# mLSTM cross-attention and spiking FFN: another order of all steps, and normalisation offsets column by column

## What is computed

```python
def _mlstm_cell(q, k, v, ...):              # q = layernorm(x), k = v = ctx
    ifg = concatenate([q, k, v], -1)
    ig, fg = ifg @ igate_w.T + igate_b, ifg @ fgate_w.T + fgate_b   # 8 heads
    cs = cumsum(log_sigmoid(fg), 1)
    log_D = where(tril, cs[:, :, None] - cs[:, None, :], -inf) + ig[:, None, :]
    m = max(log_D, -1)
    C = (qh @ kh.T) / sqrt(32) * exp(log_D - m)
    h = C / (maximum(abs(C.sum(-1)), exp(-m)) + 1e-6) @ vh
    return layernorm(h) * ln_scale
x = x + tanh(g_xattn) * _mlstm_cell(layernorm(x), ctx, ctx)

def _L0_ffn_ref(x):                         # x = layernorm(x)
    y = square(relu(x @ W_fc.T)) @ W_proj.T             # 256 -> 1024 -> 256
    # 5 steps: mem = 0.9 * mem + y - (mem > 1); spikes += (mem_new > 1)
    return sum(spikes) / 5
x = x + tanh(g_ffn) * _L0_ffn_ref(layernorm(x))
```

## Time and profile before

| | |
|---|---|
| median of 3 runs | 650.81 us (650.64 to 652.63) |
| profiled execution | 652.49 us |
| its span in the trace | 650.7 us |
| busy: PE / DVE / POOL / ACT | 90% / 83% / 75% / 74% |
| mean granted clock of TensorE | 0.978 |
| moved by DMA | 71.33 MB, 110 GB/s |

### The profile page before, as it was taken

One profiled execution on the slowest core, in us unless ns is written; L12 is line 12 of the kernel. 1 busy time (PEld: TensorE's weight loads), 2 busy tenths in 40 slices (PEclk: granted clock), 3 DMA queues, 4 the chain that ended last, 5 costly groups with the idle time before them and its releaser, 6 DMA issues.

```text
span 650.7 us, 17665 instructions
## 1 busy us (share of the span) xinstructions
PE 586.0 (90%) x6032; PEld 483.9 (74%) x6032; DVE 540.4 (83%) x1222; ACT 483.0 (74%) x1011; POOL 485.6 (75%) x531
## 2 busy tenths in 40 slices
PE   1266787799999999999999999999999999999995
PEld 0255677788787778888788878788778877787895
DVE  4878786878988899899989998899989898887444
ACT  4555676788777878888787888788887876777773
POOL 6257668887896969977997979787888788675642
PEclk9997798999999999999999999999999999999998
DMA  8915552745187154835476436916473507600101
GB/s 267 229 52 117 85 130 61 151 122 99 53 164 197 46 119 118 194 55 98 115 184 132 79 88 141 203 37 116 113 195 89 113 8 144 134 33 2 33 2 65
DMA packets 73192, 71.33 MB, mean 110 GB/s; under 512 B 8720, under 2 KB 68752, under 8 KB 73104
## 3 DMA queue, kind: packets, MB, share of 16 engines
q1 hardware_dynamic: 71888, 70.00, 47.3%
q10 hardware_dynamic: 1216, 0.21, 0.2%
HBM read 27.44 MB, written 8.39 MB: 55 GB/s over the span
## 4 chain that ended last, share of the span: by engine, by line
PE 61%; issue 10%; ACT 8%; DVE 7%; POOL 6%; DMA 0%; POOLq 0%; ACTq 0%; DVEq 0%
PE z_ps L1013 20%; PE y_ps L1077 18%; PE arg_ps L704 4%; PE qk_ps L719 3%; PE misc_ps L465 3%; PE misc_ps L531 2%; POOL sq_lo L1056 2%; POOL c_lo L748 2%; PE pv_ps L843 2%; PE pv_ps L766 2%; PE pv_ps L768 2%; ACT sq_hi L1035 2%; PE pv_ps L767 1%; POOL am_rest L639 1%; PE y_ps L1106 1%
## 5 line engine op out<-in xcount | busy, mean ns | idle before, releaser
L1056 POOL TENSOR_TENSOR sq_lo<-w_raw,sq_hi 128x512 fp32r<-128x512 f32 (+1 forms) x96 | 112.7, 1176 | 57.7 <-ACT w_raw L1036 56.8
L748 POOL TENSOR_TENSOR c_lo<-decay 128x512 bf16<-128x512 f32 x128 | 132.3, 1040 | 25.7 <-DVE decay L738 23.3
L1013 PE MATMUL z_ps<-x_hi,wfc_hi 128*128 128x512 f32 (+1 forms) x288 | 115.1, 400 | 3.8 <-ACT w_raw L1023 3.2
L1013 PE MATMUL z_ps<-x_hi,wfc_lo 128*128 128x512 f32 (+1 forms) x288 | 107.0, 372 | 0.0
L1013 PE MATMUL z_ps<-x_lo,wfc_hi 128*128 128x512 f32 (+1 forms) x288 | 106.9, 371 | 0.0
L738 DVE TENSOR_TENSOR decay<-qk_ps,decay 128x512 f32<-128x512 f32 x128 | 86.9, 679 | 23.3 <-PE qk_ps L719 17.1
L1077 PE MATMUL y_ps<-sq_hi,wpr_hi 128*128 128x512 f32 (+1 forms) x256 | 105.7, 413 | 0.4 <-POOL sq_lo L1056 0.4
L730 ACT ACTIVATE decay<-arg_ps,lqk_col 128x512 f32<-128x512 f32 x128 | 86.3, 675 | 19.4 <-PE arg_ps L707 18.6
L1077 PE MATMUL y_ps<-sq_lo,wpr_hi 128*128 128x512 f32 (+1 forms) x256 | 98.1, 383 | 0.0
L1077 PE MATMUL y_ps<-sq_hi,wpr_lo 128*128 128x512 f32 (+1 forms) x256 | 98.0, 383 | 0.0
L1056 POOL TENSOR_TENSOR sq_lo<-relu,sq_hi 128x512 fp32r<-128x512 f32 (+1 forms) x48 | 56.1, 1169 | 33.3 <-ACT relu L1036 33.2
(11 more groups left out here) (161 smaller groups left out, 1732.7 us busy)
## 6 DMA issues: line engine op xcount, KB each, us to landing
x_in<-x SPq DMA_DIRECT2D x32, 256.0 KB, 3.1
kT_in<-ctx_cols SPq DMA_DIRECT2D x32, 256.0 KB, 3.8
v_in<-ctx_rows SPq DMA_DIRECT2D x32, 256.0 KB, 3.2
k_stack<-kT_hi SPq DMA_DIRECT2D x64, 128.0 KB, 3.3
k_stack<-kT_lo SPq DMA_DIRECT2D x64, 128.0 KB, 3.6
q_stack<-qT_hi SPq DMA_DIRECT2D x64, 128.0 KB, 3.9
q_stack<-qT_lo SPq DMA_DIRECT2D x64, 128.0 KB, 4.1
out<-w_raw SPq DMA_DIRECT2D x32, 256.0 KB, 3.6
```

The lines of the kernel that those rows point to most:

```text
L748: e.tensor_tensor(c_lo[i % NCH][:, :], c, top(c), ALU.subtract).then_inc(sem("c_lo"), 1)
L1013: ins = e.matmul(z_ps[:, tokens(q)], lhsT, rhs, start=(n == 0), stop=(n == len(terms) - 1))
L1056: e.tensor_tensor(sq_lo[n % NSQ][:, tokens(q)], relu[n % NRE][:, tokens(q)], sq_hi[n % NSQ][:, tokens(q)].bitcast(fp32), ALU.subtract).the ...
```

## The change

First, `offset_of`, which computes -mean * rstd for each token, takes one instruction per column in place of one for the tile:

```diff
         def offset_of(e, off, mv, rstd):
-            return e.scalar_tensor_tensor(off[:, :], mv[:, :, 0], -1.0, rstd[:, :], ALU.mult, ALU.mult)
+            for t in range(off.shape[1]):
+                ins = e.tensor_scalar(off[:, t:t + 1], mv[:, t, 0:1], rstd[:, t:t + 1], -1.0, ALU.mult, ALU.mult)
+            return ins
```

Second, the five lists stand in another order. Every list has the same steps as before, each once (SP 211, ScalarE 704, VectorE 583, TensorE 806, GpSimd 514), with the same waits; the first z step that follows the ramp's set-up and the last z step stand at the same positions of TensorE's list, and TensorE's steps from job 17's z step 3 on are in the same order. A line or two of the lists:

```diff
             load_x(e, 0)
-            load_k(e, 0)
             load_x(e, 1)
             load_x(e, 2)
+            load_k(e, 0)
             load_x(e, 3)
+            setup_load_wfc(e)
...
+                load_k(e, 4 * n + 9)
                 stack_heads(e, 4 * n + 5)
-                load_k(e, 4 * n + 9)
+                load_x(e, 4 * n + 10)
                 load_values(e, 4 * n + 6)
+                load_m_rows(e, 4 * n + 6)
                 load_a_rows(e, 4 * n + 6)
-                load_m_rows(e, 4 * n + 6)
```

More of the change, by code:

```diff
@@ L1145, in sync_program @@
[L1145 to L1150, removed]
+            stack_heads(e, 0)
+            setup_load_wproj(e)
+            load_x(e, 5)
+            load_k(e, 3)
+            stack_heads(e, 1)
+            load_x(e, 6)
+            load_a_rows(e, 0)
+            load_k(e, 4)
+            load_values(e, 1)
             load_values(e, 2)
             load_a_rows(e, 1)
-            load_values(e, 3)
+            load_k(e, 5)
@@ L1691, in vector_program @@
             ln2_stats(e, 2)
+            x1_step(e, 2)
             cmul(e, 3, 0)
-            x1_step(e, 2)
-            cmul(e, 3, 1)
             gate_pre(e, 3)
@@ L2053, in tensor_program @@
             gate_products(e, 8)
+            arg(e, 5, 3)
             qk(e, 5, 2)
             y_step(e, 1, 4)
-            arg(e, 5, 3)
             for n in range(1, 6):
+                y_step(e, 2 * n - 1, 5)
+                state(e, 4 * n + 1)
                 gate_products(e, 4 * n + 5)
-                y_step(e, 2 * n - 1, 5)
                 qk(e, 4 * n + 1, 3)
@@ L2098, in tensor_program @@
                 z_step(e, 2 * n, 6)
-                arg(e, 4 * n + 3, 2)
                 gate_T(e, n + 3)
@@ L2106, in tensor_program @@
                 z_step(e, 2 * n + 1, 0)
+                state(e, 4 * n + 3)
                 qk(e, 4 * n + 3, 1)
-                state(e, 4 * n + 3)
-                floor_T(e, n + 3)
+                arg(e, 4 * n + 3, 2)
                 y_step(e, 2 * n, 6)
@@ L2194, in tensor_program @@
             z_step(e, 12, 6)
-            arg(e, 27, 2)
             gate_T(e, 9)
@@ L2202, in tensor_program @@
             z_step(e, 13, 0)
+            state(e, 27)
             qk(e, 27, 1)
-            state(e, 27)
-            floor_T(e, 9)
+            arg(e, 27, 2)
             y_step(e, 12, 6)
@@ L2237, in tensor_program @@
             pv(e, 28, 1)
+            arg(e, 29, 1)
             inter(e, 28)
-            arg(e, 29, 1)
             z_step(e, 13, 6)
             arg(e, 29, 2)
+            qk(e, 29, 1)
             y_step(e, 13, 4)
+            z_step(e, 13, 7)
             arg(e, 29, 3)
-            qk(e, 29, 1)
-            z_step(e, 13, 7)
             qk(e, 29, 2)
             y_step(e, 13, 5)
+            state(e, 29)
             qk(e, 29, 3)
@@ new lines, in gpsimd_program @@
+            c_lo_step(e, 24, 1)
+            square_lo(e, 11, 3)
+            c_lo_step(e, 24, 2)
+            c_lo_step(e, 24, 3)
+            state_lo(e, 24)
+            v_lo_step(e, 25)
+            k_weigh(e, 25)
+            square_lo(e, 11, 4)
+            k_hi(e, 29)
+            k_lo(e, 29)
+            square_lo(e, 11, 5)
+            k_weigh_lo(e, 25)
+            c_lo_step(e, 25, 0)
+            v_hi_step(e, 26)
+            square_lo(e, 11, 6)
+            square_lo(e, 11, 7)
+            c_lo_step(e, 25, 1)
@@ new lines, in gpsimd_program @@
+            state_lo(e, 25)
+            c_lo_step(e, 25, 2)
+            c_lo_step(e, 25, 3)
+            v_lo_step(e, 26)
+            c_lo_step(e, 26, 0)
+            k_weigh(e, 26)
+            k_weigh_lo(e, 26)
+            k_hi(e, 30)
+            k_lo(e, 30)
+            square_lo(e, 12, 0)
+            c_lo_step(e, 26, 1)
+            v_hi_step(e, 27)
+            square_lo(e, 12, 1)
+            c_lo_step(e, 26, 2)
+            k_hi(e, 31)
+            square_lo(e, 12, 2)
+            k_weigh(e, 27)
```

1031 lines of the change are left out of this document (497 added, 534 removed).

## The result

The changed kernel takes **630.63 us** (median of 4 runs, 630.20 to 631.39), the kernel before 651.1 in the same comparison; the ratio is 0.9685, 95% interval 0.9656 to 0.9715. That is 20.5 us faster, where I had forecast 5.5 and a range that ended at 637.7. The profiled execution took 630.20 us, its span is 628.4. The two profiled executions lie 22.3 us apart, 1.8 more than this, since that of before was one of its longer ones; the sum of the prediction, made against the same execution of before, had 7.2.

The account below looks back on a forecast made before the run. The prediction took the loop to be bound by TensorE's own work. From 652.49 us it summed offsets 0, first gates 0, splits -2.2, bank pairs -1.2 and loop -3.8 to 645.3 us, range 637.7 to 652.7.

Parts of the forecast that it names:

- The price on the path is 0: VectorE's layernorm offsets, taken column by column: 80 more instructions, some 11 us more VectorE work, no cost on TensorE's path.
- rival 3: VectorE's new column offsets are held as long as the 1075 ns cumulative sum, making the kernel slower, 665 us; chance 0.05.
- If all five turns go like the best, -3.8: Steady loop: each of five turns gains 0.76 us by matching the 70.83 us turn, 3.8 us faster together.
- the bounds are 0, and -5.9: Range for the loop's gain: nothing, up to 5.9 us if the best turn's 0.43 us without TensorE work also goes.
- v's low part behind k's: GpSimd in the loop: k's high part waits for stack DMAs, delaying v's low part; TensorE idles 1.21 us at 415.67 us.
- The ramp, -3.4: Set-up before the steady loop: weight splits moved, -2.2 us, and same-bank pairs separated, -1.2 us.
- The splits: Weight splits moved out of the first attention units in the ramp: -2.2 us, VectorE's alone, between 0 and -4.3.
- the pairs on one bank: Ramp: consecutive TensorE steps sharing the single qk_ps or arg_ps buffer are mostly separated: -1.2 us, between 0 and -3.0.
- the first gates: Ramp: mask builder moved earlier, weight splits now ahead of the gates' output; gain at most 1.6, loss 2.1, priced 0.
- the tail: End of the kernel, transposing, adding and storing: order unchanged from the last z steps on, price 0.
- the multiplication of unit 3: Sign in the ramp: this VectorE step, at 49.29 us before, would come at 47 us or earlier.
- rival 2: SP's load of x, now ahead of the stack, makes TensorE's qk wait once 2.6 us slack is used: 657 us; chance 0.11.

## Why the prediction was wrong

The direction was right, the size was not: three terms failed.

**"The price on the path is 0" of the offsets.** True for the kernel before (0.9991), and worth 16 us in the changed order, 20 with the changed order behind the old ramp. I had priced the edit against the old order and the order against the old offset, each by itself. The clue stood in the earlier trace rows: an operation on 128x2 that takes up to 1197 ns and one on 128x4 that takes 172 can't be explained by its size. I used this only for rival 3, as a risk of the new form. The right question was what a new order would do with an old form that can be held: from about one GpSimd instruction long (1.2 us) to four or five (3.7 to 4.7). The Trainium skill's rule on two SBUF inputs that I cited there speaks for the change; I let it reduce a rival and didn't price the gain. The Trainium skill's rule on the number of operations ("VectorE: DVE Perf Modes", section "Rules for kernel authors"), by which 80 more should cost, is not borne out for this change: nothing measurable in before's lists, where the prediction reckoned 11.8 us by that rule, and 26.2 us of offsets in the changed kernel against 37.2 in the same order with 80 fewer. Where the form can be held it is: 128 with two SBUF inputs took 22 us longer than 48.

**"If all five turns go like the best, -3.8", and "the bounds are 0, and -5.9".** Measured in the five turns: -9.0, and another -2.1 behind them, which I had at 0. The best turn was no floor, and TensorE's busy time was no floor either (70.44 against 69.52 us for the same matmuls). The mechanism that I named, v's low part behind k's, holds 2.7 us of the old trace, which the run with that step alone didn't give in the median. It was one wait among several (4.6 us listed in all, before), the other half of the gain lies in busy time, and both need the columns: with the old offset the new loop is 3.5 us longer than the old one.

**The ramp, -3.4.** Measured -11.2. The splits were mis-sized (-2.2, some 0 to 1.5), the pairs on one bank about right (-1.2, measured 0.5 to 1.8). What I had counted only by those pairs are the 7.9 us between the first z steps of jobs 0 and 2. There the listed waits fell from 11.4 to 6.8 us; the most of them, 6.4 us in eleven places, were relus late for the single z bank and exponentials late for arg_ps, both on ScalarE. I had looked at three waits since they stood in zero-distance pairs. Some 1.2 us of the 7.9 go with the clock, as far as the run with the new offsets in before's lists tells. Which of the moves in that stretch are worth how much stays open, beyond the pairs; with SP's old list the stretch takes 59.7 us in place of 56.1, and the first z step is 5.1 us later (72.47).

My account of the gates and splits also misread ScalarE's new list. Ahead of the first gates' output stands now the first half of `split_wfc_hi`; its second half stands between the first two outputs, and `split_wpr_hi` 0 behind both. And VectorE did not grow by 11 us, it has 3.6 less to do.

**Right were**: the first gates at about 0 (the first arg even comes 1.1 us later), the tail at 0, the multiplication of unit 3 before 47 us (46.30), rival 2's slack of 2.6 us and that it would not decide, rival 3's improbability, the offset's duration (205 ns for my 250), and that the wait at L810 would vanish.

## What to carry to other kernels

A new order and a new form of a small operation must be priced together: the order decides what stands beside the operation, and the form whether that can hold it. Where one small VectorE operation with two SBUF inputs shows a maximum several times its median, look at GpSimd's row beside it, and pass the small operand as a per-partition scalar, column by column if need be. The shortest turn of a loop and an engine's busy time are no floors. And lists that are tuned together can't be mixed freely: GpSimd's new list alone cost 33 us here (38 with the old offset), SP's old list in the new kernel 42.

## What the runs showed of the hardware

A VectorE operation with two inputs in SBUF waited through four GpSimd tensor_tensor instructions in a row (3.7 us), and in four cases of three runs through five (4.7 to 5.0 us), though each of those ends in between; more often it was let in after one. With one tensor input of one element per partition the same product took 180 to 215 ns in 105 cases in which a GpSimd tensor_tensor was running; with one input of 32x128 it was held for 1.2 us, six times in the kernel before.

The granted clock of a profile can miss. In the changed kernel the record says 0.50, the 1.2 GHz level, for 50 to 69 us; in the run with v's step set back, whose lists are the same up to there, it says 1.00. First the stretch (columns of the earlier trace rows) and one group of the timeline of the changed kernel, then both of the other:

```profile
50.00:69.00 19.00, 14.15 (x178) 12.61 (x179) 17.28 (x49) 11.72 (x26) 14.44 (x17) 0.50 0.40 96
```

```profile
57.00 1.06 PE L467 MATMUL misc_ps<-ident,xln 128*128 128x128 f32 x4
```

```profile
50.00:69.00 19.00, 14.15 (x178) 12.53 (x179) 17.92 (x51) 12.44 (x27) 14.25 (x16) 1.00 0.41 95
```

```profile
57.08 1.06 PE L467 MATMUL misc_ps<-ident,xln 128*128 128x128 f32 x4
```

Four transpositions take 1.06 us in both, and 0.66 at full speed (L465 at 305.86 above, granted 1.00), after the same matmuls and pauses. So TensorE is at the lower level in both. Neither lost a thing by the other's record: the first z step starts at 67.38 and 67.47 us. The duration of like groups is the better clock.
